# Router exponentials from tanh: one activation function exchanged, three VectorE instructions added per gate

## The reference

```
x = x + tanh(g_xattn) * conv_attention(ctx, ctx, layernorm(x), ssm_kernel, D)
x = x + tanh(g_ffn)   * moe(layernorm(x), Wg, W1, W3, W2, sw1, sw3, sw2)
```

```
probs = softmax(xt @ Wg);  eidx = argmax(probs);  gate = probs[eidx]
pos   = number of earlier tokens that chose the same expert
keep  = pos < 256;  flat = eidx * 256 + pos  (dropped if not keep)
h  = silu(xd @ W1) * (xd @ W3);  oe = h @ W2
out = oe[flat] * gate * keep + (silu(xt @ sw1) * (xt @ sw3)) @ sw2
```

## Time and profile before

| | |
|---|---|
| median of the runs | 230.75 us (230.36, 230.75, 231.74) |
| the profiled execution | 230.07 us |
| its span, first to last instruction | 228.3 us |
| TensorE busy | 197.4 us (86% of the span) |
| VectorE busy | 149.6 us (66%), 483 instructions |
| GpSimd busy | 127.2 us (56%) |
| ScalarE busy | 80.6 us (35%), 153 instructions |
| TensorE's granted clock, mean | 0.989 of full speed |

### The profile page before, as it was taken

The page is one execution under the profiler, slowest core; times in us unless marked ns, Lnnn a source line. Parts: engine busy times, 40 slices in busy tenths (PEclk is TensorE's granted clock), DMA queues, the critical chain, the costliest instruction groups (busy, mean ns, idle before and its releaser), DMA issues.

```text
span 228.3 us, 3954 instructions
## 1 busy us (share of the span) xinstructions
PE 197.4 (86%) x1344; PEld 178.5 (78%) x1344; DVE 149.6 (66%) x483; ACT 80.6 (35%) x153; POOL 127.2 (56%) x129
## 2 busy tenths in 40 slices
PE   0295799977999899899998968997989999999970
PEld 0264679956999798888998958896889999999960
DVE  5749878599788987479863844762457655666230
ACT  2331521535542571222331473631253444234200
POOL 3796946177755489524491207064045667777652
PEclk9999999999999999999999999999999999999995
DMA  3779993000000020020310099995464897522221
GB/s 112 265 216 354 372 409 133 0 0 4 3 3 0 0 93 3 0 93 3 138 46 3 0 305 362 354 357 186 134 185 119 267 292 237 180 79 82 67 80 46
DMA packets 24101, 31.87 MB, mean 140 GB/s; under 512 B 3390, under 2 KB 21574, under 8 KB 24080
## 3 DMA queue, kind: packets, MB, share of 16 engines
q1 hardware_dynamic: 21424, 24.75, 32.6%
q0 software_dynamic: 2304, 6.05, 7.9%
q10 hardware_dynamic: 352, 0.81, 1.0%
HBM read 21.32 MB, written 10.54 MB: 140 GB/s over the span
## 4 chain that ended last, share of the span: by engine, by line
PE 64%; DMA 9%; DVE 9%; issue 5%; ACT 5%; POOL 4%; POOLq 1%; ACTq 0%; SPq 0%; DVEq 0%
PE fb L1144 13%; PE tp L1083 10%; PE z L1144 10%; PE z L1058 9%; PE z L1168 8%; PE z L1055 5%; PE fb L1168 5%; DVE terms L452 3%; DMA kskip_scratch<-kp 3%; DMA toep<-kskip_scratch 2%; DVE stats L822 2%; PE tp L1179 2%; POOL xd_scratch L638 1%; ACT xrow L676 1%; POOL rstd L578 1%
## 5 line engine op out<-in xcount | busy, mean ns | idle before, releaser
L452 DVE TENSOR_TENSOR terms<-z,qr 128x512 f32<-128x512 f32 (+2 forms) x192 | 48.9, 323 | 10.4 <-PE z L1058 10.3
L1058 PE MATMUL z<-kv,toep 128*128 128x288 f32 x128 | 42.4, 414 | 0.0
L433 POOL TENSOR_TENSOR kv<-ct 128x768 f32<-128x768 f32 x15 | 28.1, 1875 | 15.4 <-PE z L1058 14.7
L1144 PE MATMUL fb<-xTh,wh_gu 128*128 128x256 f32 (+1 forms) x104 | 32.4, 311 | 0.7 <-issue 0.7
L1055 PEld LDWEIGHTS z<-kv,toep 128*128 128x128 f32 x128 | 22.6, 194 | 12.1 <-issue 8.1
L1055 PE MATMUL z<-kv,toep 128*128 128x144 f32 x128 | 27.5, 298 | 4.4 <-DVE terms L452 3.6
L653 POOL DMA_INDIRECT kv<-base_scratch,tok x16 | 22.4, 1398 | 15.7 <-DMA base_scratch<-x_sb 11.1
L638 POOL DMA_INDIRECT xd_scratch<-xrow,dest x16 | 17.0, 1065 | 24.8 <-DVE dest L903 21.2
L1144 PE MATMUL fb<-xTl,wh_gu 128*128 128x256 f32 (+1 forms) x104 | 29.0, 279 | 0.0
L1144 PE MATMUL fb<-xTh,wl_gu 128*128 128x256 f32 (+1 forms) x104 | 29.0, 279 | 0.0
L605 POOL TENSOR_TENSOR terms<-terms 128x512 f32<-128x512 f32 x16 | 20.2, 1280 | 11.3 <-DVE terms L452 11.3
(11 more groups left out here) (121 smaller groups left out, 377.9 us busy)
## 6 DMA issues: line engine op xcount, KB each, us to landing
terms<-w SPq DMA_DIRECT2D x16, 352.0 KB, 4.2
ct<-ctxt SPq DMA_DIRECT2D x3, 768.0 KB, 7.5
xd_scratch<-xrow SPq DMA_DIRECT2D x4, 516.0 KB, 9.5
kv<-xd_scratch SPq DMA_DIRECT2D x8, 258.0 KB, 3.2
out<-x_sb SPq DMA_DIRECT2D x8, 256.0 KB, 2.3
base_scratch<-x_sb SPq DMA_DIRECT2D x8, 256.0 KB, 2.8
terms<-w SPq DMA_DIRECT2D x8, 256.0 KB, 4.7
x_sb<-x SPq DMA_DIRECT2D x3, 512.0 KB, 6.3
```

What stands on the lines that cost most here:

```text
L433: eng.tensor_tensor(dst, left, right, ALU.mult)
L452: return eng.tensor_tensor(view(terms, t0 + row * TROW + col, [[64, 2], *td]), view(src, zo, [[512, 2], *zd]), view(qr, q0 + qo, [[CW, 2], ...
L1058: mm = pe.matmul(z[s % 2][:, k, 0:KVH], toep[:, h, 0:P], view(kv, o, [[1, KVH]]), start=False, stop=True, skip_group_check=True)
L1144: mm = pe.matmul(bank[0:rows(blk, c), m * 256:(m + 1) * 256], wt[w % 2][:, col:col + rows(blk, c)], xt[:, place, k, first:first + 256], st ...
```

## The change

The activation in `exponentials` becomes Tanh with the scale 0.5, so `ex` holds t = tanh(y/2). In `gate` VectorE computes from it 1 - t, its reciprocal, the sum over the eight experts, and then 2 * sum - 8, which is the sum of (1 + t)/(1 - t) = exp(y), since (1 + t)/(1 - t) = 2/(1 - t) - 1. The rest of `gate` stays. The buffer `t3` was there before and is used by `slot_of_token` behind the gate.

```diff
@@ exponentials(g), ScalarE
-                act.activation(ex[:, :, :], sh[:, :, :], ACT.Exp).then_inc(exp_done, 1)
+                act.activation(ex[:, :, :], sh[:, :, :], ACT.Tanh, scale=0.5).then_inc(exp_done, 1)
@@ gate(g), VectorE
                 dve.wait_ge(exp_done, g + 1)
-                chain(dve.tensor_reduce(se[:, :], ex[:, :, :], AX_X, ALU.add))
+                chain(dve.tensor_scalar(t3[:, :, :], ex[:, :, :], -1.0, 1.0, ALU.mult, ALU.add))
+                chain(dve.reciprocal(t3[:, :, :], t3[:, :, :]))
+                chain(dve.tensor_reduce(se[:, :], t3[:, :, :], AX_X, ALU.add))
+                chain(dve.tensor_scalar(se[:, :], se[:, :], 2.0, -float(E), ALU.mult, ALU.add))
                 chain(dve.reciprocal(gp[:, :], se[:, :]))
```

## The result

The changed kernel took 233.53 us (median of 8 runs, 231.72 to 236.28), the kernel before on the same chip 230.89 us (8 runs, 229.42 to 232.01). The ratio is 1.0087 (95% interval 1.0050 to 1.0124), that is +2.0 us, between +1.2 and +2.9. So the change is a small loss. The two medians stand 2.6 us apart; the ratio, by which this text goes, leaves out one execution in a slower state (236.28). It was right in sign and in that the difference stays within 1%, but short by about 1 us, and the rest of this text is about that microsecond. On the prediction's own base of 230.75 us the ratio gives 232.8, just inside its range (229.5 to 232.9).

The account below looks back on a forecast made before the run. TensorE, with the transfers it waits for, was taken to bound the kernel; 0.80 + 0.80 - 2.01 + 0 + 1.30 = +0.9 us, so 231.0 profiled and 231.6 for the median (chance 0.45), range 229.5 to 232.9.

Parts of the forecast that it names:

- What is taken away: ScalarE in the router: eight table loads go, 10.3 us; only group 2's pays, its silu 2.81 us earlier.
- What is added: VectorE in each gate: three chained instructions, two 128x32 (one a reciprocal) and one 128x4, 0.80 us per gate.
- d: VectorE time added to each gate, 0.22 + 0.37 + 0.21 = 0.80 us, between 0.65 and 0.86.
- Gates 0 and 1: TensorE pays +0.80 at group 0's wait for L897, and +0.80 through gate 1's scatters and folds on GpSimd.
- rival 3: Gate 1's delay is not passed on to TensorE; sum +0.1, 230.9 us; chance 0.09.
- Gate 2: Group 2: the loads' removal less the added gate work, -2.81 + 0.80 = -2.01 us for TensorE.
- Gate 3: Group 3's scatters: d costs 0, as the second scatter is held by VectorE's L954 and ends as now.
- Rival 2: With d over 0.85, L954 holds GpSimd's first scatter, fourth issued +1.29 later; 232.2 us; chance 0.14.
- Transfers: Last scatter lands more slowly while expert weights still arrive: +1.30 us, bounds 0 and 2.0.
- The lag: Seen from the scatters, the expert weights' queue drains 2.0 us later than now.
- The slope of 0.41 us per us: Landing time per us of lag, between two scatters around the drain at about 153; prices the lag at 0.8.
- After 160 the stream is TensorE's own and shifts whole: Behind the first expert's rows at about 160, TensorE's remaining work shifts by the sum, nothing added.

Follow-up runs that it names:

- tanh_only: Kernel before with only the activation changed to Tanh of the half, the gate's old sum left (output not the reference's): 233.13 us, ratio 1.0033.
- folds_ahead: Changed kernel with the scatters of groups 0 to 2 issued later on GpSimd, behind the next group's folds: 234.15 us, ratio 1.0103.
- after_again: The changed kernel run once more, unaltered, for a second trace: 234.44 us, ratio 1.0109.
- places_first: Changed kernel with the places put ahead of the gate in VectorE's queue: 234.17 us, ratio 1.0083.
- after: The changed kernel itself, as first measured and profiled: 233.53 us, ratio 1.0087 against the kernel before.
- ops_only: Kernel before with Exp and all loads kept and three VectorE instructions of the same shapes added to each gate: 233.51 us, ratio 1.0092.
- after_all: Changed kernel with weights of experts 3 and 4 behind earlier experts' rows, places ahead of gate, scatters behind folds: 227.09 us, ratio 0.9873.
- after_late: Changed kernel with the weights of experts 3 and 4 issued after the rows of experts 0 and 1: 231.91 us, ratio 0.9998.
- before_all: Kernel before with the same three moves (two experts' weights later, places ahead of gate, scatters behind folds): 228.13 us, ratio 0.9878.

## Why the prediction was right or wrong

- **What is taken away** (eight loads, of which only group 2's pair is worth something): right. The silu came 2.84 us earlier, seen from the rows, for 2.81. `tanh_only` bounds what all eight are worth to TensorE: 2.3 us at 138, while 10.3 us of ScalarE's time went. The Trainium skill, "ScalarE: Activation LUTs", section What ACT_TABLE_LOAD costs, adds a drain to each load; the trace doesn't agree, since the pair went and 2.84 us went with it, which the two loads of 1.28, the shorter exponential and the overlaps account for.
- **What is added** (d = 0.80): right, 0.80 in the trace. The reciprocal was put at 0.33 and took 0.353 us. The price by the operation's own row of 4 elements came near; the plain 128x32 row (0.18) would have been half.
- **Gates 0 and 1** (+0.80 each): right, +0.80 at 78 (0.77 still at 93) and 1.54 at 122 (forecast 1.60). `folds_ahead` shows that the second goes through scatters and folds on GpSimd; rival 3 falls.
- **Gate 2** (-2.01): right. From +1.54 to -0.50 is -2.04. The start at 138 was forecast 0.41 earlier and came 0.50 earlier. The wait at L1096 is gone.
- **Gate 3** (0, second scatter held by L954): right, with a narrow margin: the first scatter started at 150.29, VectorE's L957 at 150.32, and the second scatter took 1.21 in place of 2.02. The last one was issued at the same 154.38. Rival 2 would have begun 0.03 us further on; the forecast said 0.05. That it didn't come is in part luck at such a margin, though the order was the same in `after_again` (0.26 us apart), `places_first` and `folds_ahead` (0.03 and 0.06). The gate does cost TensorE 0.55 us at 149.89, where it waits for VectorE's L916 behind the gate, but that goes unseen in its wait for the rows.
- **Transfers** (+1.30, bounds 0 and 2.0): the mechanism was right, the size was not. The landing grew by 2.05, a little over the upper bound, and the read by 0.10. The lag itself was forecast well. SyncE began the weights 1.9 us later (133.63 for 131.73) against a last scatter that was issued at the same time. The last weight was issued at 145.81 for 142.93 and landed 8.4 us after that in place of 9.1, so at 154.2 for 152.0, and the share of the DMA engines fell 2.0 later. The step that failed is the price of that lag, "I take the middle of the two, +1.30": the last scatter paid all of it. It did so in all five traces with such a lag and all weights in place: counted in the same way, lags of 1.7 to 2.0 us cost 2.05 to 2.3 of landing (after, `after_again`, `tanh_only`, `places_first`, `folds_ahead`). The slope of 0.41 us per us was measured from the drain at 153, which is where the weights of the kernel before end; but stores and the scatters themselves keep the engines at 1.02 from 154 to 155 and 0.70 from 155 to 156, so the burst that the last scatter meets ends later than that.
- **"After 160 the stream is TensorE's own and shifts whole":** wrong in this execution and in `after_again` (not in `places_first`, whose twelve matmuls took 2.59). After the wait of 2.85 us TensorE ran at half its clock, +1.68 us. The sum had no term for the clock, though the grown waits were forecast. The Trainium skill, "TensorE: Matmul & The Clock Gate", section HAM oscillation — how this bites in real kernels, says that a wait for transfers may throttle the engine, so that the work behind it starts at the lower clock. The trace agrees, with the 0.50 in the window from 163; it would have been a rival of +1.7.

Put together for the profiled executions: forecast +0.9; the landing and the read +0.85 more; and 0.06 for the last scatter, which less the late start came 0.35 earlier and not 0.41. That makes the 1.8 at the first rows. With the 0.35 of the start and the 1.68 of the clock it is 3.8. The median of the runs lies below that (+2.0 by the ratio), so either the runs after don't all pay for start and clock in full, or those before pay in part as well (their median is 0.8 above the profiled execution); how often each happens wasn't measured. That the result is still inside the range is luck in part: the range's upper end was put there for rival 2, which didn't happen, and what filled it was the full landing and the clock.

## What to carry to other kernels

A saving ahead of a fixed burst of transfers is not kept, if what it brings forward must land behind that burst: find out when the DMA engines come free before you count the gain, and move the burst, not the work. Here moving two experts' weights on SyncE gained 1.5 us against the kernel before, in either kernel, where the change by itself lost 2.0. And where a change lengthens a wait of TensorE, price the clock that may fall behind it beside the wait itself: here the clock fell behind six of eight waits of 2.5 to 3.7 us, and where the twelve matmuls came next it cost them 1.7 to 2.3 us.

## What was not expected of the hardware

- TensorE's clock. From the first gate on the profiles hold eight waits of over 2.5 us. Behind six of them the granted clock fell: 2.52 (`ops_only`), 2.74 and 3.35 (`folds_ahead`), 2.85 (after), 3.22 (`after_again`), 3.71 (`tanh_only`); twelve matmuls took 4.3 to 4.9 us in place of 2.59 where they came next. Behind 2.51 and 2.91 (`places_first`) it stayed whole, with 2.59 for the twelve. No wait of up to 1.8 us there did this. Early on, all but one of the profiles wait 2.0 to 3.1 us, at 22 to 25 us; behind it the clock fell in six of them, that of after among them, and not in five others of 2.1 us. It accounts for most of the 0.35 us by which after was late before the router: from the end of this wait to the next TensorE took 8.90 us (22.67 to 31.57), before 8.61 (22.59 to 31.20). What decides between them stays open; filling a wait with other matmuls wasn't tried.
- VectorE's small operations beside GpSimd's: 128x32 operations took 1.04 and 1.75 us in place of 0.19 while GpSimd ran its fold and L433 (`after_all`), a 128x4 tensor_scalar 1.51 in place of 0.23 (`folds_ahead`). The Trainium skill, "GPSIMD Engine Reference", in its table of specifications, says that GpSimd shares its SBUF interfaces with VectorE and that the two contend when VectorE has two SBUF inputs or runs in a 2-port mode. The rows of `after_all` agree for two inputs; L885 of `folds_ahead`, one input of 4 elements, was held as well, and whether it ran in a 2-port mode no row says. The hold works in both directions here: L954 also held a scatter of GpSimd for 1 us.
- A landing of four indirect DMAs, 2.4 to 2.9 us on engines that were partly free, took 4.9 to 5.1 with the engines full (times of the last of the four, from issue). A read of rows took 6.82 behind two experts' weights (`after_late`), and 2.7 to 2.8 without.
- The first 70 microseconds, which the change doesn't touch, vary by up to 2.6 us between executions (the common row of GpSimd at 67.82 before, 68.17 after, 67.51 in `before_all`, 70.13 in `places_first`). Two spans can't be compared to less than that without such a common row ahead of the change.
